# An attention and gated FFN kernel on one core: query rope rows in two buffers, rope and weight steps placed anew

## What is computed

```
q = (x @ wq).reshape(b, s, H, QH)              # QH = NOPE + ROPE = 128 + 64
q_nope, q_pe = q[..., :NOPE], q[..., NOPE:]
kva = x @ wkv_a                                # LORA + ROPE = 64 + 64 columns
ckv = rms_norm(kva[..., :LORA]) * kv_norm_scale
k_nope, v = split((ckv @ wkv_b).reshape(b, s, H, NOPE + VD))
q_pe, k_pe = _rope(q_pe, cos, sin), _rope(kva[..., LORA:], cos, sin)
scores = concat(q_nope, q_pe) . concat(k_nope, k_pe) * scale, causal
out = (softmax(scores) @ v).reshape(b, s, H * VD) @ wo
return x + out * silu(ffn(layernorm(x)))
```

## Time and profile before

| | |
|---|---|
| median of 3 runs | 1090.41 us |
| profiled execution | 1087.01 us, its span 1085.2 us |
| mean granted TensorE clock | 0.96 of full |
| set-up, to the first scores | 0 to about 70 us |
| 128 units | about 70 to 970 us, a pair about 112 us |
| FFN tail | the rest, PE nearly without a gap |
| DMA packets | 591979, 170.24 MB, mean 157 GB/s |

### The profile page before, as it was taken

The page is one execution under the profiler, slowest core; times in us unless marked ns, Lnnn a source line. Parts: engine busy times, 40 slices in busy tenths (PEclk is TensorE's granted clock), DMA queues, the critical chain, the costliest instruction groups (busy, mean ns, idle before and its releaser), DMA issues.

```text
span 1085.2 us, 26363 instructions
## 1 busy us (share of the span) xinstructions
PE 965.5 (89%) x10560; PEld 829.1 (76%) x10560; DVE 758.7 (70%) x1095; ACT 757.9 (70%) x1093; POOL 793.0 (73%) x576
## 2 busy tenths in 40 slices
PE   5659798999889989999999899999899987989998
PEld 5637687788778777877787787877787776877887
DVE  5748578787878687768786787778677875852134
ACT  1428687788778787878787878878688875863222
POOL 3667979697969796979697969887788889623331
PEclk7869999999999999999999999999899998989999
DMA  5019999999999999999999999999999999992001
GB/s 170 10 49 168 161 188 170 195 172 175 172 194 165 177 176 193 178 172 176 193 174 170 186 183 181 168 170 182 189 148 187 178 171 211 201 166 79 1 20 59
DMA packets 591979, 170.24 MB, mean 157 GB/s; under 512 B 574064, under 2 KB 585968, under 8 KB 591856
## 3 DMA queue, kind: packets, MB, share of 16 engines
q1 hardware_dynamic: 587376, 167.89, 86.6%
q10 hardware_dynamic: 4480, 0.66, 0.4%
HBM read 15.41 MB, written 2.10 MB: 16 GB/s over the span
## 4 chain that ended last, share of the span: by engine, by line
POOL 34%; PE 30%; SPq 9%; DMA 9%; issue 6%; DVE 6%; ACT 5%; ACTq 1%; POOLq 0%
POOL hl L1114 16%; PE s_ps L529 10%; PE s_ps L627 9%; DMA pT<-hl 5%; SPq L472 5%; PE slot_ps L529 4%; POOL pe L1114 4%; POOL q_swap L1114 3%; SPq L464 3%; POOL QB_lo L1114 2%; POOL QA_lo L1114 2%; ACT hl L733 2%; POOL QB_hi L1114 2%; POOL QA_hi L1114 2%; DMA q_swap<-q_pe 2%
## 5 line engine op out<-in xcount | busy, mean ns | idle before, releaser
L1114 POOL TENSOR_TENSOR hl<-prob,hl 128x1024 f16<-128x1024 f32 (+4 forms) x256 | 417.5, 1631 | 134.0 <-ACT hl L733 120.1
L806 ACT ACTIVATE prob<-s_ps,neg_max 128x1024 f32<-128x1024 f32 (+7 forms) x384 | 317.5, 861 | 71.3 <-DVE neg_max L948 44.2
L733 ACT ACTIVATE hl<-prob 128x1024 f16<-128x1024 f32 (+7 forms) x384 | 296.3, 804 | 79.2 <-DMA pT<-hl 76.5
L945 DVE TENSOR_REDUCE part_max<-s_ps 128x1 f32<-128x1024 f32 (+7 forms) x256 | 244.6, 986 | 142.2 <-PE s_ps L627 124.2
L643 PE MATMUL o_ps<-v,pT 128*128 128x65 f16 x2176 | 228.7, 193 | 18.8 <-DMA pT<-hl 14.2
L644 PE MATMUL o_ps<-v,pT 128*128 128x64 f16 x2176 | 229.1, 196 | 0.0
L645 PE MATMUL o_ps<-v,pT 128*128 128x65 f16 x2176 | 227.8, 192 | 0.0
L643 PEld LDWEIGHTS o_ps<-v,pT 128*128 128x128 f16 x2176 | 204.5, 97 | 20.9 <-DMA pT<-hl 15.3
L954 DVE TENSOR_TENSOR hl<-prob,hl 128x1024 f16<-128x1024 f32 (+3 forms) x128 | 190.1, 1485 | 37.9 <-ACT hl L733 36.4
L645 PEld LDWEIGHTS o_ps<-v,pT 128*128 128x128 f16 x2176 | 203.9, 99 | 0.0
L644 PEld LDWEIGHTS o_ps<-v,pT 128*128 128x128 f16 x2176 | 203.2, 97 | 0.0
(11 more groups left out here) (183 smaller groups left out, 1950.3 us busy)
## 6 DMA issues: line engine op xcount, KB each, us to landing
q_swap<-q_pe SPq DMA_DIRECT2D x128, 64.0 KB, 2.2
pT<-hl SPq DMA_TRANSPOSE x256, 5.1
wq_sb<-in_L_attn_wq_dram SPq DMA_DIRECT2D x8, 384.0 KB, 4.2
acc<-in_L_attn_x_dram SPq DMA_DIRECT2D x4, 512.0 KB, 6.3
wo_sb<-in_L_attn_wo_dram SPq DMA_DIRECT2D x8, 256.0 KB, 3.4
x_in<-in_L_attn_x_dram SPq DMA_DIRECT2D x1, 2048.0 KB, 9.6
out_dram<-y SPq DMA_DIRECT2D x8, 256.0 KB, 2.1
wkvs<-in_L_attn_wkv_b_dram SPq DMA_DIRECT2D x8, 128.0 KB, 4.0
```

What stands on the lines that cost most here:

```text
L733: return nc.scalar.activation(dst, src, ACT.Copy)
L806: nc.scalar.activation(prob_of(u, m), score_bank(u, m), ACT.Exp, bias=neg_max[:, r:r + 1]).then_inc(exp_done, 1)
L945: nc.vector.tensor_reduce(part_max[:, u % 2, m:m + 1], src, AX.X, ALU.max).then_inc(part_done, 1)
L1114: return lambda: nc.gpsimd.tensor_tensor(dst, a, b, op)
```

## The change

- `q_pe` has two copies, used by n mod 2; ACT's copy for n waits for the swap and the rope step .0 of n - 2 instead of n - 1. `pe_b` has one copy in place of two; ACT's copy into it for n waits for POOL's step "B lo" of n - 1 instead of n - 2.
- SP issues `turn_first` of a unit before the swap, not behind it.
- PE: in the first unit of a pair the scores of m = 1 stand behind the weighing of m = 0.
- POOL's steps are placed anew. rope g.0 of groups 1 and 0 moves from k = 3 and 11 to 4 and 12, g.1 and g.2 from 4 and 12 to 5 and 13; the splits of A1 from 5 to 6, B2lo from 5 to 6, B1 from 6 to 7, A0 from 13 to 14, B3lo from 13 to 14, B0 from 14 to 15. `wpe_hi` moves from 6 to 3 and `wpe_lo` from 6 to 4. ACT's `rope_of_b` moves from 6 to 7 (group 1) and from 14 to 15 (group 0).
- Last pair: the FFN load and its POOL steps come one unit later, the FFN job of k = 7 goes to 13, and the output job outP1b moves into the tail.

```diff
-FFN_COUNT = {7: 1, 8: 1, 9: 2, 10: 2, 12: 1, 14: 2, 15: 2}
+FFN_COUNT = {8: 1, 9: 2, 10: 2, 12: 1, 13: 1, 14: 2, 15: 2}
...
-POOL_FFN = {4: ["up_zero", "up_scale_zero", "down_zero"], 6: ["up_scaled0"], 7: ["up_scaled1"], 8: ["down_scaled"]}
-
-ROPE_B_OWN, ROPE_B_NEXT = {4: 2, 6: 1}, {12: 3, 14: 0}
...
+ROPE_B_OWN, ROPE_B_NEXT = {4: 2, 7: 1}, {12: 3, 15: 0}
...
-        q_pe = ab("q_pe", [P, BANK])
+        q_pe = ab("q_pe", [P, 2, BANK])
...
-        pe_b = ab("pe_b", [LORA, 2, BANK])
+        pe_b = ab("pe_b", [LORA, BANK])
...
                 pair, k = divmod(u, PU)
+                turn_first(u)
                 for name in jobs_at(u - 1):
                     if name[0].startswith("qB"):
                         swap(int(name[0][2:]), name[1])
-                turn_first(u)
                 turn_rest(u)
...
-                if pair == PAIRS - 1 and k == 4:
+                if pair == PAIRS - 1 and k == 5:
                     load_ffn()
...
+                first = (u + 1) % PU == 0
                 if u + 1 < NU:
                     scores(u + 1, 0)
-                    scores(u + 1, 1)
+                    if not first:
+                        scores(u + 1, 1)
                 if u >= LAG:
                     weigh(u - LAG, 0)
                 if u + 1 < NU:
+                    if first:
+                        scores(u + 1, 1)
                     scores(u + 1, 2)
...
-                    if n >= 1:
-                        before = GROUP_ORDER[(n - 1) % NG], (n - 1) // NG
-                        act.wait_ge(swapped, 64 * n)
+                    if n >= 2:
+                        before = GROUP_ORDER[(n - 2) % NG], (n - 2) // NG
+                        act.wait_ge(swapped, 64 * (n - 1))
                         act.wait_ge(pool_done, POOL.after((f"rope{before[0]}.0", before[1])))
-                    copy(q_pe[h * ROPE:(h + 1) * ROPE, :], ps[0:ROPE, :])
+                    copy(q_pe[h * ROPE:(h + 1) * ROPE, n % 2, :], ps[0:ROPE, :])
...
-                if n >= 2:
-                    before = GROUP_ORDER[(n - 2) % NG], (n - 2) // NG
+                if n >= 1:
+                    before = GROUP_ORDER[(n - 1) % NG], (n - 1) // NG
                     act.wait_ge(pool_done, POOL.after((f"B{before[0]}lo", before[1])))
-                copy(pe_b[:, n % 2, :], pe[ROPE:P, n % 2, :]).then_inc(rope_b, 1)
+                copy(pe_b[:], pe[ROPE:P, n % 2, :]).then_inc(rope_b, 1)
```

More of the change, by code:

```diff
@@ L132 @@
 JOBS_FIRST = {0: ["qA2"]}
-FFN_COUNT = {7: 1, 8: 1, 9: 2, 10: 2, 12: 1, 14: 2, 15: 2}
+FFN_COUNT = {8: 1, 9: 2, 10: 2, 12: 1, 13: 1, 14: 2, 15: 2}
 EARLY = {PU * PAIRS - 1: (0, 2), PU * PAIRS: (2, 4)}
-OUT_LAST = {j: (name, PAIRS - 1) for j, name in ((0, "outT2"), (1, "outP2a"), (2, "outP2b"), (5, "outT3"), (7, "outP3a"), (8, "outP3b"))}
+OUT_LAST = {j: (name, PAIRS - 1) for j, name in ((0, "outP1b"), (1, "outT2"), (2, "outP2a"), (3, "outP2b"), (5, "outT3"), (7, "outP3a"), (8, "outP3b"))}
 def jobs_at(u):
@@ L191 @@
     (r, 0) for r in side("B", 3) + rope(0) + side("B", 0)]
-POOL_NEXT = {1: ["wkvs"], 6: ["wpe_hi", "wpe_lo"], 9: rope(3)[:1], 10: rope(3)[1:], 11: rope(0)[:1] + side("A", 3), 12: rope(0)[1:] + ["B3hi"],
-             13: ["B3lo"] + side("A", 0), 14: side("B", 0)}
-POOL_OWN = {1: rope(2)[:1], 2: rope(2)[1:], 3: rope(1)[:1] + side("A", 2), 4: rope(1)[1:] + ["B2hi"], 5: ["B2lo"] + side("A", 1), 6: side("B", 1)}
-POOL_FFN = {4: ["up_zero", "up_scale_zero", "down_zero"], 6: ["up_scaled0"], 7: ["up_scaled1"], 8: ["down_scaled"]}
-ROPE_B_OWN, ROPE_B_NEXT = {4: 2, 6: 1}, {12: 3, 14: 0}
+POOL_NEXT = {1: ["wkvs"], 3: ["wpe_hi"], 4: ["wpe_lo"], 9: ["rope3.0"], 10: ["rope3.1", "rope3.2"], 11: side("A", 3), 12: ["rope0.0", "B3hi"],
+             13: ["rope0.1", "rope0.2"], 14: side("A", 0) + ["B3lo"], 15: side("B", 0)}
+POOL_OWN = {1: ["rope2.0"], 2: ["rope2.1", "rope2.2"], 3: side("A", 2), 4: ["rope1.0", "B2hi"], 5: ["rope1.1", "rope1.2"], 6: side("A", 1) + ["B2lo"],
+            7: side("B", 1)}
+POOL_FFN = {5: ["up_zero", "up_scale_zero", "down_zero"], 7: ["up_scaled0"], 8: ["up_scaled1"], 9: ["down_scaled"]}
+ROPE_B_OWN, ROPE_B_NEXT = {4: 2, 7: 1}, {12: 3, 15: 0}
 def steps_at(u):
@@ L457, in swap @@
                     a, b = slice(i * half, (i + 1) * half), slice((i ^ 1) * half, (i ^ 1) * half + half)
-                    sp.dma_start(q_swap[a, :], q_pe[b, :]).then_inc(swapped, 16)
+                    sp.dma_start(q_swap[a, :], q_pe[b, n % 2, :]).then_inc(swapped, 16)
             def turn_first(u):
@@ L1136, in rope_step @@
                     done = ((queries_split, n - 1),) if 2 <= n < 4 else ()
-                    run((name, pair), tt(turned, q_pe[:], cosT[:, query_cols(g)], ALU.mult), (hi_done, after("hi", (f"qB{g}", pair))),
+                    run((name, pair), tt(turned, q_pe[:, n % 2, :], cosT[:, query_cols(g)], ALU.mult), (hi_done, after("hi", (f"qB{g}", pair))),
                         (tables_loaded[g], 32), *done)
@@ L1146, in split_step @@
                 n = group_no(g, pair)
-                src = (pe_b if head else pe)[0:ROPE, n % 2, :]
+                src = pe_b[:] if head else pe[0:ROPE, n % 2, :]
                 hi, lo = queries(Q_hi, head, g)[0:ROPE, :], queries(Q_lo, head, g)[0:ROPE, :]
```

## The result

The changed kernel takes 1063.95 us (median of 4 runs, 1061.47 to 1066.10) against 1090.62 us before; the ratio is 0.975, 95% interval 0.971 to 0.979. The profiled execution took 1065.26 us, with a span of 1063.5. The forecast was 1066.

A forecast was written before the change was run, and what follows sets the result against it. Nearly equal engines, PE busiest, bound by its standstills and their aftermath. First halves 18 us, pair 0 1 and pair ends 5 make 24; 1087.0 - 24 = 1063, plus 3.4 for the median, gives 1066; range 1044 to 1091.

The forecast's parts named there:

- Where PE stands still, and that equal engines leave little of a saved wait: Engines are nearly equally busy, so PE's standstills and what follows count; at most 7.7 us a pair, plus clock, to win.
- The ceiling of 46 us: The most PE could get back: 17 (q_pe), 13 (weight step), 5 (pair ends) and 11 us (clock).
- q_pe twice, 17 us of PE: ACT's 26.4 us of waits for the swap go; 64% of that, 17 us, becomes PE time.
- Weight step, 12.8 us: With wc_hi and wc_lo made in units 3 and 4, PE's 12.8 us of stalls on wc_lo go.
- Pair ends, 5 us: Weighing fills PE's idle time before the second score block in a pair's first unit: 0.73 us at 7 pair ends.
- Later half of a pair, nothing but the pair ends: POOL's steps of units 11 to 15 are spread likewise; only the 5 us at the pair ends were counted.
- Clock, 11 us: Slow matmuls follow about half of 14 PE stalls; avoiding these low clock stretches gives back 11 us.
- Levelled steps: POOL's work in a pair is unchanged, only spread more evenly, limiting the first half's gain to 2.6 us a pair.
- POOL's unbroken row: POOL works without a gap from 428.07 to 473.59 in pair 3, so unit 57 can begin 2.6 us earlier at most.
- pe_b, 7.0 us of wait a pair: In unit 7 ACT's copy into the single pe_b newly waits for POOL's B2lo, at worst 7.0 us a pair.
- Swap, zero: Low transpose goes 2.5 us earlier in four units a pair, swap some 2 us later; counted as zero.
- the zero that the prediction gave it: POOL steps beside DVE's subtractions could each cost up to 0.6 us more, or as much less; left at zero.

The follow-up runs named there:

- first experiment: The changed kernel with pe_b in two copies again, q_pe staying in two: 1065.18 us, 0.976 of the kernel before.
- third experiment: The changed kernel with the swap issued ahead of the low transpose again, q_pe in two copies: 1061.37 us, 0.974 of the kernel before.
- eighth: The changed kernel with POOL's rope and split steps, pe_b copies and last pair's FFN pieces placed as before: 1090.78 us, 1.000 of the kernel before.
- eleventh experiment: The kernel before with rope and split steps, pe_b copies and last pair's pieces placed as changed, weight step left in unit 6: 1065.55 us, 0.978.
- experiment 54: Not a run: 54 and 55 there are unit numbers, whose low halves start 9.7 us apart in the eleventh experiment.

## Why the prediction came out right, and where its working did not

The time, 1066 forecast and 1064 measured, was right. The way there was right only in part.

*Where PE stands still, and that equal engines leave little of a saved wait.* Right. The ceiling of 46 us was not reached, and each saved wait alone showed it: two q_pe gave 5 us and the weight step gave none.

*q_pe twice, 17 us of PE.* This term failed. It took 64% of each saved wait of ACT as won by PE, from one stall of one pair. Measured: 5 us by itself (0.996), and nothing on top of the levelled steps, where 1061.37 us with two copies stands against 1060.55 with one. What the second q_pe does in the changed kernel is to pay for the swap's new place, which without it costs 43 us.

*Weight step, 12.8 us.* Failed as a term of its own: 1.003 alone, and 1064.95 against 1065.55 us on the levelled steps with one q_pe. In the changed kernel's own setting it is worth 13 us, though not by the stall on wc_lo, which does not come back when it is undone. What the step is worth depends on what stands beside it.

*Pair ends, 5 us.* Mis-sized: 1.8 us or nothing.

*Later half of a pair, nothing but the pair ends.* This is where the sum was most wrong. It had 2.6 us from the first half of a pair, 18 and 1 in all, and less than 1 from the second. Measured, the second half gives 2.4 us and the first 0.6. POOL's steps of units 11 to 15 moved just as those of units 3 to 6 did, and the working gave them no term. That 24 us came near the 27 measured is therefore luck: too much in one half, too little in the other.

*Clock, 11 us.* Half seen: PE's busy time, which carries the clock, fell by 4.7 us in the profiled execution. The gain does not hang on it: with two pe_b (first experiment) PE is busy 965.5 us in the profiled execution, as before, and that execution takes 1067.16. Of the 180 windows of 5 us between 60 and 960 us, 22 had a granted clock under 0.95 before and 12 have one now, but also 20 in the third experiment, whose kernel is as fast.

*Levelled steps.* The step that bounded them was near in its numbers and wrong in its reading. I worked out that unit 54's low half would start 2.8 us earlier; counted from wkvs it was 2.2. I worked out that POOL's unbroken row lets unit 57 begin 2.6 us earlier; it was 1.2. B2lo was to end 35.7 us behind wkvs (463.8 - 428.07); it ended at 456.18 - 419.93 = 36.25. (The row of before also had a gap of 0.22 us that I overlooked.) But I took the steps' new places as the limit on what other edits could win, when they were the source: the eighth and eleventh experiments show that without them nothing is won, and that alone they win 25 us. The working had noted 76.5 us of ACT's waits for transposes and then gave them no term.

*pe_b, 7.0 us of wait a pair.* The wait came where it was placed, in all eight units 7, but it is 2.1 to 4.5 us long. In pair 3 it is 3.00, since ACT came to the copy 33.3 us behind wkvs (453.27 - 419.93) and not 28.7: the transposes hold it, 2.2 us ahead of a high half of unit 53 among others. And it costs nothing (first experiment). That it would eat most of what the other terms gave, which brought the sum down to 24, was not so; two errors, terms that were too large and a limit put on the wrong cause, met.

*Swap, zero.* Right with two q_pe (0.974 against 0.975), far off without.

What the runs show is that the places of POOL's steps are the cause. How they act is in part argued. A low half on POOL, the issue of its transpose and the landing are a chain with two units of slack, as `prob`, `hl` and `pT` have two copies. Before, three to four steps in each of units 3 to 6 stood between the low halves. POOL's timeline of the kernel before, the low halves of units 52, 53 and 61:

```profile
443.13 3.13 POOL L1114 TENSOR_TENSOR hl<-prob,hl 128x1024 f16<-128x1024 f32 x2
...
450.78 3.75 POOL L1114 TENSOR_TENSOR hl<-prob,hl 128x1024 f16<-128x1024 f32 x2
...
506.48 3.63 POOL L1114 TENSOR_TENSOR hl<-prob,hl 128x1024 f16<-128x1024 f32 x2
```

The low halves of units 54 and 55 are at 458.89 and 466.75. From unit 52 to unit 55 they start 7.65, 8.11 and 7.86 us apart, while a pair of 111 us has 7 us for a unit. So POOL falls behind by up to a microsecond a unit. With steps moved to later units, the low halves in the middle of the stretch come sooner: unit 54's starts 30.8 us behind wkvs before, 28.6 in the changed kernel and 26.7 in the eleventh experiment, where 11, 10 and 8 steps stand ahead of it. In the second half it is alike: unit 61's low half starts 30.3 us behind unit 57's before (506.48 - 476.21) and 27.2 now (494.05 - 466.84):

```profile
494.05 2.13 POOL L1119 TENSOR_TENSOR hl<-prob,hl 128x1024 f16<-128x1024 f32 x1
```

It is not the evenness of the steps that acts. In the changed kernel units 53 and 54 are 6.5 us apart, but 54 and 55 are 7.8; in the eleventh experiment 54 and 55 are 9.7 us apart, more than anywhere in this stretch before, and it is as fast. Nor do the summed waits tell one story: ACT waits for the transposes longer in the changed kernel (94.0 us after 76.5) and less in the eleventh (67.5), at times within 2 us of each other. Which wait carries the gain stays open.

The Trainium skill, "GPSIMD Engine Reference", section "8. Key points", names contention of GpSimd with VectorE instructions that have two SBUF inputs. POOL's busy time went from 793.0 to 791.2 us with the same instructions, so the new places did not add to it, and the zero that the prediction gave it holds.

## What to carry to other kernels

Where several engines are nearly equally busy, find the chain that has the least slack and count when each of its links starts, unit by unit, over the whole period and not only in the half where the stalls catch the eye. Move the side work that stands ahead of it to a later place, as far as its readers allow, before giving other waits a second buffer. A wait that is removed elsewhere can come back as another: test each edit alone and each left out, since two edits may be worth almost nothing singly (here -5 and +2 us), and one may only repair what another broke. A DMA that someone waits for soon should not be moved behind a transpose on the same queue: SP takes 1.3 to 3.7 us to issue a low transpose in the trace of before.

## What the runs showed that I had not expected

The order of two DMA issues on SP is worth 43 us of 1060 (1103.75 against 1060.55) where the tile that the swap reads, q_pe, has one copy, and nothing that can be measured (1063.95 against 1061.37) where it has two. And in the changed kernel 1.5 us of POOL work a pair at another place costs 13 us, while on the kernel before, with the other steps moved, the same place costs nothing (1065.55 against 1064.95). Small edits here do not add up.
